# Layer norm's epsilon, scale and mean moved from VectorE to GpSimd in a gated cross-attention block

## The reference

```python
def _layernorm(x, axis=-1, eps=1e-05):
    m = jnp.mean(x, axis=axis, keepdims=True)
    v = jnp.var(x, axis=axis, keepdims=True)
    return (x - m) / jnp.sqrt(v + eps)

x = x + jnp.tanh(g_xattn[0]) * xattn(ctx, _layernorm(x), mask, b)   # queries = _layernorm(x) / sqrt(32)
x = x + jnp.tanh(g_ffn[0]) * ffn(_layernorm(x), w_gate, w_up, w_down)
# ffn: (silu(n @ w_gate.T / 127) * (n @ w_up.T / 127)) @ w_down.T / 127
```

## Time and profile before

| | |
|---|---|
| time of before, median of 3 runs | 154.86 us (154.65 to 155.37) |
| the profiled execution | 154.62 us, its span 152.6 us |
| busy, share of the span | PE 90%, VectorE 78%, ACT 60%, GpSimd 59% |
| granted clock of TensorE | 0.996 of full |

### The profile page before, as it was taken

The page is one execution under the profiler, slowest core; times in us unless marked ns, Lnnn a source line. Parts: engine busy times, 40 slices in busy tenths (PEclk is TensorE's granted clock), DMA queues, the critical chain, the costliest instruction groups (busy, mean ns, idle before and its releaser), DMA issues.

```text
span 152.6 us, 3962 instructions
## 1 busy us (share of the span) xinstructions
PE 136.7 (90%) x1381; PEld 102.2 (67%) x1381; DVE 118.8 (78%) x315; ACT 90.9 (60%) x202; POOL 90.4 (59%) x139
## 2 busy tenths in 40 slices
PE   0999899988789969998999999999999989899970
PEld 0365667764477749875977697777787858677840
DVE  4869799999689995999999998587825957676731
ACT  3433666674757576838783877755686746575520
POOL 7243550746574893696758677634765687865530
PEclk9999999999999999999999999999999999999998
DMA  4689930000042036023552334230020020020022
GB/s 147 147 299 365 372 123 0 4 0 0 4 96 43 6 69 131 11 71 69 38 104 69 69 65 79 73 69 0 4 71 0 0 73 0 2 69 4 0 75 77
DMA packets 19936, 11.06 MB, mean 72 GB/s; under 512 B 13492, under 2 KB 19144, under 8 KB 19912
## 3 DMA queue, kind: packets, MB, share of 16 engines
q1 hardware_dynamic: 19872, 10.75, 27.0%
q10 hardware_dynamic: 40, 0.01, 0.0%
HBM read 5.52 MB, written 2.10 MB: 50 GB/s over the span
## 4 chain that ended last, share of the span: by engine, by line
PE 38%; DVE 27%; issue 12%; POOL 10%; ACT 7%; DMA 4%; POOLq 0%; ACTq 0%; DVEq 0%; SPq 0%
PE ps L1396 14%; PE ps L1418 7%; DVE max_cols L1068 5%; DVE norm L956 4%; PE ps L1325 3%; DVE gated L1112 3%; DVE stats L937 3%; POOL rstd L655 3%; PE ps L1331 2%; DVE h L1123 2%; ACT probs L792 2%; DMA n_t<-norm 2%; DMA mask_row<-in_mask_BxS_ik_dram 2%; PE ps L1345 2%; PE ps L1301 2%
## 5 line engine op out<-in xcount | busy, mean ns | idle before, releaser
L1396 PE MATMUL ps<-n_t,w_gu_t 128*128 128x256 f16 x384 | 49.9, 273 | 2.5 <-DMA n_t<-norm 1.3
L1396 PEld LDWEIGHTS ps<-n_t,w_gu_t 128*128 128x128 f16 x384 | 36.1, 98 | 12.2 <-DMA n_t<-norm 3.0
L701 POOL TENSOR_TENSOR h<-h 128x256 f16<-128x256 f32 x48 | 32.2, 671 | 19.1 <-ACT h L849 18.9
L1418 PE MATMUL ps<-w_d_t,h 128*128 128x256 f16 x192 | 28.3, 272 | 0.3 <-POOL h L701 0.2
L840 ACT ACTIVATE tanh_h<-ps 128x256 f32<-128x256 f32 x48 | 18.3, 381 | 15.4 <-PE ps L1396 15.0
L1112 DVE SCALAR_TENSOR_TENSOR gated<-tanh_h,ps 128x256 f32<-128x256 f32 x48 | 19.8, 413 | 6.7 <-ACT tanh_h L840 6.6
L1068 DVE TENSOR_REDUCE max_cols<-ps 128x4 f16<-128x512 f32 x32 | 21.4, 682 | 3.5 <-PE ps L1267 3.3
L655 POOL TENSOR_TENSOR rstd<-var_eps,neg_half 128x2 f32<-128x2 f32 x16 | 11.3, 703 | 19.9 <-DVE var_eps L944 19.8
L849 ACT ACTIVATE h<-h 128x256 f16<-128x256 f32 x48 | 19.8, 413 | 4.4 <-DVE h L1123 4.4
L792 ACT ACTIVATE probs<-ps,exp_bias 128x512 f32<-128x512 f32 x32 | 21.7, 682 | 0.7 <-PE ps L1303 0.3
L1123 DVE SCALAR_TENSOR_TENSOR h<-ps,gated 128x256 f32<-128x256 f32 x48 | 20.4, 424 | 1.7
(11 more groups left out here) (89 smaller groups left out, 201.5 us busy)
## 6 DMA issues: line engine op xcount, KB each, us to landing
x_sb<-in_x_dram SPq DMA_DIRECT2D x8, 256.0 KB, 8.7
out_dram<-x_sb SPq DMA_DIRECT2D x8, 256.0 KB, 2.1
kv<-in_ctx_dram SPq DMA_DIRECT2D x4, 256.0 KB, 6.4
w_raw<-in_L_ffn_w_gate_dram SPq DMA_DIRECT2D x1, 768.0 KB, 7.5
w_raw<-in_L_ffn_w_up_dram SPq DMA_DIRECT2D x1, 768.0 KB, 9.3
w_raw<-in_L_ffn_w_down_dram SPq DMA_DIRECT2D x1, 768.0 KB, 8.1
q_stacks<-q_parts SPq DMA_TRANSPOSE x8, 3.3
n_t<-norm SPq DMA_TRANSPOSE x4, 3.0
```

The source lines that it names most:

```text
L701: pool.tensor_tensor(h16[:, r % 2, m, 1, :], h32[:, n % NHB, :], h16[:, r % 2, m, 0, :], ALU.subtract).then_inc(h_low, 1)
L1396: ins = pe.matmul(dst, lhs, rhs, start=(w == 0 and (k, l) == terms[0]), stop=(k, l) == terms[-1], skip_group_check=True)
L1418: ins = pe.matmul(dst, lhs, rhs, start=(m == 0 and t == 0 and l == 0), stop=(m == MT - 1), skip_group_check=True)
```

## The change

VectorE ends its share of a `stats` step with the second `bn_aggr`, which now signals `var_ready`. GpSimd makes `var_eps` itself, waits on a new semaphore of its own, `var_eps_ready`, and then takes the power. Where GpSimd normalises it subtracts the mean in `mv`, so `neg_mean` is gone. A new wait of VectorE on `var_ready` protects the one `stats` tile: the `bn_stats` of a step wait until the `bn_aggr` of the step before are done.

```diff
@@ gpsimd, step stats
                         pool.wait_ge(var_ready, place + 1)
+                        pool.tensor_scalar(var_eps[:, place % NLB, :], mv[:, place % NLB, :, 1], LN_EPS,
+                                           1.0 / Q_SCALE_SQ if step[1] == 1 else 1.0, ALU.add, ALU.mult
+                                           ).then_inc(var_eps_ready, 1)
+                        pool.wait_ge(var_eps_ready, place + 1)
                         pool.tensor_tensor(rstd[:, place % NLB, :], var_eps[:, place % NLB, :], neg_half[:, :],
                                            ALU.pow).then_inc(rstd_ready, 1)
@@ gpsimd, steps norm1 and norm2 (the same edit in both)
                             ins = pool.tensor_scalar(norm32[:, slot, i, :], x_sb[:, 2 * r + i, :],
-                                                     neg_mean[:, slot, i:i + 1], rstd[:, slot, i:i + 1],
-                                                     ALU.add, ALU.mult)
+                                                     mv[:, slot, i, 0:1], rstd[:, slot, i:i + 1],
+                                                     ALU.subtract, ALU.mult)
@@ vector, step stats
                             wait_normed(dve, before)
+                        if place:
+                            dve.wait_ge(var_ready, place)
                         for i in range(2):
                             mine(dve.bn_stats(stats[:, i, :], x_sb[:, 2 * r + i, :]))
                         wait_mine()
                         for i in range(2):
-                            mine(dve.bn_aggr(mv[:, slot, i, :], stats[:, i, :]))
-                        wait_mine()
-                        if which == 2 or norm1_on_pool((step[0].replace("stats", "norm1"), r)):
-                            dve.tensor_scalar(neg_mean[:, slot, :], mv[:, slot, :, 0], -1.0, None, ALU.mult)
-                        dve.tensor_scalar(var_eps[:, slot, :], mv[:, slot, :, 1], LN_EPS,
-                                          1.0 / Q_SCALE_SQ if which == 1 else 1.0, ALU.add, ALU.mult
-                                          ).then_inc(var_ready, 1)
+                            ins = dve.bn_aggr(mv[:, slot, i, :], stats[:, i, :])
+                        ins.then_inc(var_ready, 1)
```

More of the change, by code:

```diff
@@ L357, in flamingo_block_kernel @@
         rstd = sb("rstd", [P, NLB, 2], F32)
-        neg_mean = sb("neg_mean", [P, NLB, 2], F32)
         mask_raw = sb("mask_raw", [B * NC, P], I32)
@@ L436, in flamingo_block_kernel @@
         var_ready, rstd_ready = sem("var_ready"), sem("rstd_ready")
+        var_eps_ready = sem("var_eps_ready")
         normed1, normed2 = sem("normed1"), sem("normed2")
```

## The result

The changed kernel takes 169.93 us (168.66 to 171.79, 4 runs) against 154.79 us of before (154.65 to 155.37): ratio 1.0943, 95% interval 1.0874 to 1.1012. By the ratio it is 14.6 us slower, where 154.0 us was forecast, in a range of 153.3 to 155.5.

A forecast was written before the change was run, and what follows sets the result against it. TensorE's own pace bounds 90 to 120 us, with VectorE also near full from 60 to 75; elsewhere savings count only through TensorE's waits. Seven places sum to -0.83 us, against 154.86 giving 154.0 us, range 153.3 to 155.5.

The forecast's parts named there:

- fourth rival: GpSimd's new small instruction costs more than 0.20 us where powers are waited for; middle 155.7 us, chance 0.15.
- 1, start: Start: VectorE's first two norms lose 0.10 us each waiting for the power, the third's power comes 0.10 late; +0.30 us.
- 2: 34 to 38 us, two neighbouring steps: the norms of GpSimd and VectorE each gain 0.06 us; -0.06 us.
- 3: 47 to 57 us, path to TensorE's 1.28 us DMA wait: VectorE 0.27 us earlier, power 0.10 later; -0.17 us.
- 4: 64 to 72 us: VectorE's norm goes ahead of GpSimd's low part and ends 1.0 us earlier, shortening TensorE's gaps; -0.85 us.
- 5: A round later the order turns too, but TensorE has only a gap of 0.25 us there; -0.15 us.
- 6: 90 to 125 us: TensorE's own pace, so VectorE's savings become idle time; 0.
- 7, last step: Near 130 us: GpSimd is busy until var_eps can start, and its norm decides ACT's next tanh; +0.10 us.
- The turn: Near 67 us VectorE's norm begins before GpSimd's low part, taking about 1.2 us in place of 1.94.

The follow-up runs named there:

- experiment 1: Kernel before with only the sign changed: VectorE writes the mean itself into neg_mean, GpSimd's norms subtract and multiply; 167.05 us, ratio 1.0795.
- Experiment 4: Changed kernel with add and mult in the norms; GpSimd makes var_eps, then neg_mean for the 10 steps that need it; 157.05 us, ratio 1.0135.
- experiment 10: Kernel of Experiment 4 without DMA transposes for the second norm, all eight parts turned by TensorE; ratio 1.0081 against the kernel before.
- 9: Kernel before without DMA transposes for the second norm, all eight parts turned by TensorE and copied by ACT; ratio 1.0099.
- 6: Kernel before with a second instruction like var_eps, its output unread, and a wait for it ahead of each power on GpSimd; 158.42 us, ratio 1.0174.
- 3: Changed kernel, but VectorE still makes neg_mean and GpSimd's norms add and multiply again; 157.08 us, ratio 1.0167.
- experiment 2: Kernel before with neg_mean written in place into mv, from where GpSimd adds it; ratio 1.0024.
- experiment 11: Kernel before without epsilon and scale: VectorE makes no var_eps, GpSimd takes the power of the variance itself; 154.22 us, ratio 0.9943.

## Why the prediction was wrong, by its own steps

**The subtraction.** The step that failed is "The edit to the subtraction I cost at nothing: same operands, same two operations per column". The price of a `tensor_scalar` on GpSimd does not go by the number of operations: 0.55 us for (add, mult), 1.22 for (subtract, mult). In the trace of experiment 1 the 20 norms take 25.1 us in place of 11.1, and 12.3 us reach the end of the kernel (1.6 us of the profiled execution through TensorE's clock, as above). For the round shown, nothing stands beside the path of norm, high part, low part, turn and TensorE; the other rounds were not followed one by one. The prediction did name the sign ("if GpSimd's subtraction takes longer than 0.55 us"), and its fourth rival had the right engine, "GpSimd's chain becomes the bound", with a chance of 0.15, but priced the wrong instruction; the sentence on a slower subtraction carried no size. No row of before had a second pair of operations on GpSimd at this width. The nearest, the subtraction of two tiles on the same 256 columns (0.67 us, L701), asks for 0.12 us more a norm, 2.4 us in all; the measured 0.67 more a norm, 13.4 us in all, makes 168 us.

**The new instruction and the waits.** Right: 0.20 us, 0.08 to 0.10 us for its own wait, 0.36 to 0.38 us from aggregation to power; VectorE goes on 0.17 us behind the start of the pair. By the Trainium skill's factor of two for elementwise work on GpSimd ("GPSIMD Engine Reference", "Performance versus the Vector engine") `var_eps` would be 0.33 us, an estimate; the trace has 0.20. For the norm, (subtract, mult) on 256 columns took 1.23 us on GpSimd and 0.40 us on VectorE where nothing held it up, a factor of 3, and (add, mult) 0.55.

**The places, with add kept.** The subtraction hides what the rest of the sum was worth. Experiment 4 is the change without it, and experiment 10 against 9 the same without DMA transposes of the second norm. TensorE runs the same matmuls in the same order in each pair, so one can read how much later the same matmul begins. What that lateness gains or loses in each stretch, in us, from single executions:

| place of the prediction | until, us | forecast | experiment 4 less before | 10 less 9 |
|---|---|---|---|---|
| 1, start | 25 | +0.30 | +1.15 | +1.02 |
| 2 | 42 | -0.06 | +0.54 | +0.53 |
| 3 | 58 | -0.17 | +0.02 | +0.02 |
| 4 | 75 | -0.85 | +0.40 | -1.10 |
| 5 | 90 | -0.15 | +0.06 | -0.51 |
| 6 | 126 | 0 | 0.00 | 0.00 |
| 7, last step | end | +0.10 | +0.54 | +0.52 |
| sum | | -0.83 | +2.7 | +0.5 |

**Place 4, -0.85 us.** The turn was right and its worth wrong. The pair of 1.94 us took 1.08 to 1.09 us at both places in experiments 4, 6 and 10, close to the 1.05 us of the earlier trace rows, and in experiment 4 the waits of 0.24 and 0.44 us at L1260 and L1325 are gone. What failed is "TensorE's own gaps bound what comes of it": it left out the next wait. The matmuls behind L1325 read the part that the DMA turns. In the trace of before it was issued at 69.25 and in at 72.31, and its reader begins with no time to spare:

```profile
72.38 0.77 PEld L1396 LDWEIGHTS ps<-n_t,w_gu_t 128*128 128x128 f16 x8 [0.41 <-DMA n_t<-norm]
72.39 1.05 PE L1396 MATMUL ps<-n_t,w_gu_t 128*128 128x256 f16 x8
```

No time of TensorE's could be won there, and every 0.1 us of GpSimd's lateness was lost. In experiment 4 the transpose was issued 2.15 us later, and a wait stands in front of the same matmuls:

```profile
74.49 1.05 PE L1405 MATMUL ps<-n_t,w_gu_t 128*128 128x256 f16 x8 [1.25 <-DMA n_t<-norm]
```

The 0.85 us were won and 1.25 lost, together the +0.40 of the table. Experiments 3 and 6 have waits of 2.0 (0.9 of it the slow transpose) and 1.0 us there. Without the DMA the turn was worth 1.1 us (10 against 9), more than forecast. The prediction read the matmuls' rows alone, which name the DMA once; the weight loads name it four times:

```profile
PEld ps L1396 <- DMA n_t<-norm: 3.0, 4, 1.8
```

Three of the four are 0.41 us. That is a place to look and not a lost time: in front of part 4 the load has the same 0.41 us, at 101.87, though the part had been in at 101.70.

**Place 5, -0.15 us.** The same: +0.06 with the DMA transpose, -0.51 without. The "gap of 0.25 us" that it counts stands at 106.08 in the trace of before; near 87 us the gap is 0.09.

**Places 1, 2 and 7, +0.34 us together.** Too small. At place 2 three small instructions and two powers follow each other on GpSimd in experiment 4. VectorE's norm waited 0.28 us for the second power and took 1.23 us beside GpSimd's norm in place of 1.05, and the wait of TensorE behind it grew. The rows before and in experiment 4:

```profile
38.68 0.40 PE L1260 MATMUL ps<-k_stacks,q_stacks 128*128 128x128 f16 x4 [0.61 <-DVE max_cols L1068]
```

```profile
40.37 0.40 PE L1269 MATMUL ps<-k_stacks,q_stacks 128*128 128x128 f16 x4 [1.15 <-DVE max_cols L1077]
```

Experiments 3 and 6 lose 0.4 and 0.5 us in the same stretch, experiment 2, which moves nothing, none. At the last step the traces of 3, 4, 6 and 10 lose 0.2 to 0.5 us where 0.10 was forecast. At the start a single trace says little: the third `stats` step began 0.7, 0.4 and 0.8 us later in experiments 2, 3 and 4, and experiment 2 moves nothing there; executions of one kernel differ by as much. Only the 0.4 us that experiments 4 and 10 lose between 20 and 23 us, at the third norm, stand out from that (0.10 forecast). **Place 3** gained nothing, where 0.17 us was forecast.

**The whole.** Of 14.6 us, 12.3 are the subtraction (experiment 1). The move with add kept is 2.1 us (experiment 4); without the DMA transposes it is -0.3 us, with an uncertainty of about 0.7 us from the two intervals (9 and 10). The two together are 14.4 us, if they add.

## What to carry to other kernels

The price of an instruction on GpSimd is read for the exact pair of operations, operands and width; an algebraically equal form can cost twice as much, so a sign kept in a small tile by an engine that seems busier may be cheap. Ahead of each wait that is to be shortened, look at what the waiting engine needs next, the weight loads' rows too: where a transfer is in time by some hundredths, an earlier matmul wins nothing and a later producer loses at once. Time taken off the busiest engine beside TensorE, with the power earlier by it, was worth 0.9 us of some 2 where nothing was put elsewhere (experiment 11: 0.20 us for each of 6 steps, 0.07 for each of 10), and less than nothing when 0.3 us were put ahead of each power. To see which places of a sum failed, compare the start of the same matmul in two traces, stretch by stretch.

## What the runs showed of the hardware

On GpSimd, `tensor_scalar` with two pointers on 128x256 f32: 0.55 us for (add, mult) and (mult, add), 1.22 to 1.23 us for (subtract, mult), (mult, subtract), (subtract, add) and (max, min), 0.92 us for subtract alone; where the pointer lies made no difference (0.56 us in experiment 2). A VectorE norm of two tiles and GpSimd work on SBUF hold each other up piece by piece: 0.73 us with GpSimd idle (11.77 us of before), 1.05 to 1.23 us beside two norms of GpSimd, 1.94 us beside two low parts. A DMA transpose of 256 rows took 3.0 to 3.1 us from issue to landing in most cases, 3.5, 3.9 and 4.7 to 4.8 us in some executions. TensorE's granted clock fell from 2.4 to 1.2 GHz for 3.4 us at a time behind waits of 1.44, 2.36 and 2.38 us in the changed kernel, not behind others of 1.40, 1.55 and 1.85 us; in the profiled execution of before, with 1.28 us as its longest wait in the middle, it fell only at the end.
